# First slots of attention without the ring copy, weights' low parts on GpSimd, last feed-forward unit in two halves

## The chip, the cores and the metric

The kernel runs on one core of a Trainium2 chip. The metric is the device time of one execution in microseconds (us); the time given for a kernel is the median of several runs.
## The reference

A transformer block over 16 sequences of 256 rows and 256 features, in float32:

```
h = layernorm(x, ln1);  x = attention(h, h, sa_*) + x        # 16 heads of 64
h = layernorm(x, ln2);  x = attention(h, cond, ca_*) + x     # cond: 256 rows of 192 features
h = layernorm(x, ln3);  p = h @ ff_w1 + ff_b1                # 256 -> 2048
x = (p[:, :1024] * gelu(p[:, 1024:])) @ ff_w2 + ff_b2 + x    # 1024 -> 256
attention: softmax(q k^T / 8) v per head, heads joined, then @ wo + bo
```

## The kernel before

Each operand of a matrix product is split in two parts that the fast product format holds exactly: a high part (rounded) and a low part (the value less the high part). A product of two operands is the sum of three: high·high, high·low, low·high.

**Slots.** Both attentions are one loop of 256 slots (ATT), a slot being a pair of heads of one sequence; 128 slots for self-attention, 128 for cross-attention. The loop is written out by hand for each engine as one function per slot (`pe_slot`, `act_slot`, `dve_slot`, `pool_slot`, and the loop in the SyncE block); engines meet at semaphores only, and each works its list strictly in order. In slot c TensorE computes, in this order: scores of slot c (`pe_scores`), Q and K of slot c+3 (AHEAD, line 318), V of slot c+1 (line 294), output projection of slot c-4 (line 337), transposes of the probabilities of slot c-1 (line 350), probabilities times V of slot c-2 (line 364). ScalarE rounds Q/K (line 466) and does the exponentials (line 457) and the high part of the transposed probabilities (line 479); VectorE makes the low parts of Q/K (line 593), the negated maxima (line 557) and the low probabilities (line 545, `dve_p_low`; head 1 of slot c-2 early in the slot, head 0 of slot c-1 late); GpSimd splits V (726, 728), next sequence's rows, the output and some weights.

**The ring.** After the split, QKS holds for two heads (rows 0 to 63 and 64 to 127) the tiles K high, Q high, Q or K low. `copy_ring` copies these by four DMAs per slot to RX (lines 398 and 400), so that each head has a 128-row operand: own rows hold the head's high part, the other 64 rows the other part. With it a head's scores take two 128-row products per 128 queries (lines 280 and 281) instead of three of 64 rows. The copies for slots 1 and on are issued by SP; for slot 0 head 1 by ACT. `pe_scores` waits for them (d_dup).

**The start.** The self-attention weights come as 12 pieces of 256 KB (`PIECES`: matrix q, k or v, and quarter; `load_weights`, line 958). ScalarE rounds each into the high part (`act_weights`, line 971), VectorE makes each low part (`dve_weights`, lines 982 and 984), in numerical order, counted by s_wlo. Q/K of the first sequence wait for their pieces, V too. Slots -3 to -1 do Q/K of slots 0 to 2 and V of slot 0. TensorE runs transposes of the identity without use (`pe_warm`) at the start, before slot -3 ends and at slot 0. The second sequence's rows are normalized by VectorE in slot 0 and go through HBM; ScalarE loads them back (line 406).

**The end.** The feed-forward part has 64 units: 8 chunks (2 sequences) times 8 slices of 128 hidden features. Unit c: 12 first-layer products of 512 columns (line 828, 6 for the value half and 6 for the gate half), GELU on ScalarE (878), multiply, high and low part on VectorE (920, 924, 926); then 12 second-layer products of unit c-1 (841). After a chunk VectorE adds the residual in two halves (934) and SP stores two sequences (1052).

Of the kernel before, what the change touches and what calls it, by code (L numbers as in the profile page):

```python
# [11 lines left out]
P = 128  # L12
# [26 lines left out]
AHEAD = 3  # L39

# [34 lines left out]
def block_kernel(nc, x, ctxt, ln1_g, ln1_b, ln2_g, ln2_b, ln3_g, ln3_b, sa_wq, sa_wk, sa_wv, sa_wo,  # L75
                 sa_bo, ca_wq, ca_wk, ca_wv, ca_wo, ca_bo, ff_w1, ff_b1, ff_w2, ff_b2, out):
    ctx = ExitStack()
    with ctx:
# [75 lines left out]
        def pieces_for(m, p):  # L154

            return PIECES.index((m, p // 2)) + 1
# [18 lines left out]
        s_wlo = sem("s_wlo")  # L175
        s_ph = sem("s_ph")
# [89 lines left out]
        def pe_warm(e, times, bank=WOP):  # L266

            for _ in range(times):
                e.transpose(bank[:, S:S + P], IDN[:, :], IDN[:, :])
# [14 lines left out]
        def pe_values(e, sl, v):  # L284
# [5 lines left out]
            if v < PAIRS and v % 2 == 0:  # L290
                e.wait_ge(s_wlo, pieces_for(2, v))
# [6 lines left out]
        def pe_slot(e, sl):  # L298
            c = sl.c
            if sl.has(c + AHEAD):  # L300
# [3 lines left out]
                if k < PAIRS and k % 2 == 0:  # L304
                    e.wait_ge(s_wlo, pieces_for(1, k))
# [14 lines left out]
                last.then_inc(a.pe_qk, 1)  # L320

# [20 lines left out]
            if sl.has(c - 1):  # L342
                s = c - 1
                sl.wait(e, a.act_exp, 2 * s + 2)
                for i in range(2):
                    sl.wait(e, a.dve_pl, 2 * s + i - 1)
                    for kt in range(TT):
                        for qt in range(TT):
                            q0 = (i * TT + qt) * S + kt * P
                            last = e.transpose(PTB[:, i, kt * S + qt * P:kt * S + (qt + 1) * P],  # L350
                                               PT[:, s % 2, q0:q0 + P], IDN[:, :])
                last.then_inc(a.pe_t, 1)
# [38 lines left out]
        def copy_ring(e, k, *heads):  # L391
# [3 lines left out]
            if k >= 2:  # L395
                e.wait_ge(a.pe_s, 2 * (k - 1))
            for i in heads:
# [28 lines left out]

        def act_slot(e, sl):
# [21 lines left out]

            if sl.has(c):  # L450
                sl.wait(e, a.pe_t, c - 1)
                sl.wait(e, a.dve_rc, c - 1)
                for i in range(2):
# [6 lines left out]

            if sl.has(c + AHEAD):
                k = c + AHEAD
                sl.wait(e, a.pe_qk, k + 1)
                if k > 1:
                    e.wait_ge(d_dup[k % 2], 16 * COPIES * (k // 2))
                e.activation(QKS[:, k % 2, 0:2, :], qk_bank(k)[:, :].rearrange("p (u s) -> p u s", u=2), ACT.Copy) \  # L466
                    .then_inc(a.act_hi, 1)
# [79 lines left out]

        def dve_slot(e, sl):
# [11 lines left out]
            if c == 0:  # L560
                dve_weights(e, 6)
                e.wait_ge(a.pe_h, 2)
                dve_normalize(e, sl, a, 1, (near(1),))
# [26 lines left out]
            if sl.has(c + AHEAD):  # L590
                k = c + AHEAD
                sl.wait(e, a.act_hi, k + 1)
                e.tensor_tensor(QKS[:, k % 2, 2:4, :], qk_bank(k)[:, :].rearrange("p (u s) -> p u s", u=2),  # L593
                                QKS[:, k % 2, 0:2, :].bitcast(F32), ALU.subtract).then_inc(a.dve_lo, 1)
# [215 lines left out]

        def pe_ffn(e, sl):
# [3 lines left out]
            if sl.has(c):  # L815
# [8 lines left out]
                for g in range(2):  # L824
                    n = 0
                    for k in range(KD):
                        for wp, ap in ((0, 0), (0, 1), (1, 0)):
                            last = e.matmul(AG[c % 2][:, g, :], w1(k, wp, g * FF + f * P),  # L828
                                            rounded(chunk, ap, k), start=n == 0, stop=n == 5)
                            n += 1  # L830
                last.then_inc(fs.pe_f1, 1)

            if sl.has(c - 1):
# [3 lines left out]
                for t in range(2 * TT):  # L837
                    if f == 0 and t % 2 == 0:
# [31 lines left out]
        def act_ffn(e, sl):  # L870
            c = sl.c
            if sl.has(c):
# [3 lines left out]
                if c == 0:  # L876
                    e.wait_ge(a.pe_t, ATT)
                e.activation(FG[:, c % 2, :], AG[c % 2][:, 1, :], ACT.Gelu,
                             bias=B1[:, PAIRS + f:PAIRS + f + 1]).then_inc(fs.act_g, 1)
# [29 lines left out]

        def dve_ffn(e, sl):  # L910
# [6 lines left out]
            if sl.has(c):  # L917
# [11 lines left out]
            if f == 0 and c > 0:  # L929
                sl.wait(e, fs.pe_f2, c)  # L930
                sl.wait(e, fs.pl_xb, chunk)
                for h in range(2):
                    cols = sl.x_cols(chunk - 1, h * XW)
# [52 lines left out]
        def act_attention_slot(e, sl):  # L986
            act_slot(e, sl)
            if -AHEAD <= sl.c < 3:
                act_weights(e, *((4,), (5,), (6,), (7,), (8, 9), (10, 11))[sl.c + AHEAD])
            if sl.c == -3:  # L990
                copy_ring(e, 0, 1)
            if sl.c == -2:
                load_weights(e, 11)
# [5 lines left out]
        def dve_attention_slot(e, sl):  # L999
            c = sl.c  # L1000
            dve_slot(e, sl)
            if -AHEAD <= c < 3:
                dve_weights(e, *((4,), (5,), (), (7,), (8, 9), (10, 11))[c + AHEAD])
            if c == -2:
                dve_await_x(e, sl, 1)
# [307 lines left out]
```

## Time and profile before

| | us |
|---|---|
| median of 3 runs | 1729.74 (1728.88 to 1730.17) |
| the profiled execution | 1728.96 |
| its span | 1727.2 |
| TensorE busy | 1704.0 (99%) |
| VectorE busy | 1471.2 (85%) |
| ScalarE busy | 1184.5 (69%) |
| GpSimd busy | 1072.5 (62%) |

The span is the time from the first to the last thing the profile sees; a run's time is a little longer. Busy shares are means over the whole span; where an engine at 99% can still lose or win time is seen only in the stretches where it waits. All numbers below are from one profiled execution.

### The profile page before, as it was taken

To read this page: it belongs to the slowest core of one execution; us is meant where nothing else is said; L and a number is where in the kernel's file an instruction comes from. 1 tells how busy PE (TensorE), PEld (TensorE's weight loads), DVE (VectorE), ACT (ScalarE), POOL (GpSimd) and SP (SyncE) were. 2 spreads that over 40 slices of the span, in tenths; PEclk is the share of its full clock that TensorE was granted. 3 is DMA by queue.
4 is the path that set the end of the run, shared out by engine and by line. 5 is a ranking of instruction groups with operands and counts; after the bars stand their busy time and mean duration, and the time that the engine had idled before them with its cause. 6 is when DMAs were issued, how large, how long until landed. Compare 5 with 4: busy or idle time off the path is not lost.

```text
span 1727.2 us, 42949 instructions
## 1 busy us (share of the span) xinstructions
PE 1704.0 (99%) x13614; PEld 1664.4 (96%) x13614; DVE 1471.2 (85%) x3192; ACT 1184.5 (69%) x3244; POOL 1072.5 (62%) x1801
## 2 busy tenths in 40 slices
PE   7999999999999999999999999999999998999998
PEld 7999999999999999999999999999999997888887
DVE  6888889888888888899999999999999997666664
ACT  5777777777777777777777778777777775222221
POOL 3787777766666666787777777777777764132121
PEclk9999999999999999999999999999999999999999
DMA  8777777676666666667778777776666662212210
GB/s 224 195 181 177 181 177 179 172 182 164 154 157 152 158 154 161 169 165 186 188 189 192 191 189 182 183 180 168 169 168 168 161 168 53 74 50 70 65 37 25
DMA packets 287984, 265.95 MB, mean 154 GB/s; under 512 B 102416, under 2 KB 247696, under 8 KB 287760
## 3 DMA queue, kind: packets, MB, share of 16 engines
q1 hardware_dynamic: 232112, 248.18, 57.0%
q10 hardware_dynamic: 55648, 15.02, 4.0%
q8 instruction: 110, 1.80, 0.4%
q14 instruction: 114, 0.93, 0.2%
HBM read 70.40 MB, written 24.90 MB: 55 GB/s over the span
## 4 chain that ended last, share of the span: by engine, by line
PE 90%; DVE 2%; DMA 2%; ACT 1%; SPq 1%; POOL 1%; issue 1%; ACTq 0%; DVEq 0%; POOLq 0%
PE QKB L318 19%; PE PVB L364 13%; PE PTB L350 12%; PE WOP L337 10%; PE VB L294 9%; PE S L280 6%; PE S L281 6%; PE PTB L828 5%; PE S L828 5%; PE VB L841 3%; PE QKB L841 3%; DMA RX<-QKS 1%; ACT PT L457 1%; DVE NM L557 0%; ACT PH L479 0%
## 5 line engine op out<-in xcount | busy, mean ns | idle before, releaser
L457 ACT ACTIVATE PT<-S,NM 128x256 f32<-128x256 f32 x1024 | 471.1, 472 | 188.9 <-DVE NM L557 188.3
L545 DVE TENSOR_TENSOR PL<-PTB,PH 128x512 fp32r<-128x512 f32 x512 | 349.6, 683 | 89.7 <-ACT PH L479 84.0
L747 POOL TENSOR_TENSOR ON<-ON,RB 128x256 f32<-128x256 f32 x256 | 188.6, 737 | 283.9 <-DVE ON L573 270.5
L479 ACT ACTIVATE PH<-PTB 128x1024 fp32r<-128x1024 f32 x256 | 263.4, 1029 | 100.5 <-PE PTB L350 97.1
L557 DVE TENSOR_REDUCE NM<-S 128x2 f32<-128x512 f32 x512 | 325.8, 677 | 0.0
L350 PE MATMUL PTB<-IDN,PT 128*128 128x128 f32 x2048 | 266.7, 273 | 6.0 <-DVE PL L545 5.8
L280 PE MATMUL S<-RX 128*128 128x256 f32 x1024 | 257.1, 283 | 3.5 <-DMA RX<-QKS 3.3
L281 PE MATMUL S<-RX 128*128 128x256 f32 x1024 | 256.7, 283 | 0.0
L350 PEld LDWEIGHTS PTB<-IDN,PT 128*128 128x128 f32 x2048 | 229.4, 140 | 7.8 <-DVE PL L545 7.5
L337 PE MATMUL WOP<-WO,OT 128*128 128x256 f32 x1536 | 226.3, 283 | 1.2 <-POOL OT L752 1.2
L573 DVE TENSOR_TENSOR ON<-PVB,ON 64x256 f32<-64x256 f32 x512 | 213.3, 417 | 3.5
L457 ACT ACTIVATION_READ_ACCUMULATOR PT<-S,NM 128x1 f32 x1024 | 207.4, 203 | 0.0
L318 PE MATMUL QKB<-HT,WA 128*128 128x256 f32 x1512 | 203.6, 284 | 2.9 <-DVE WA L984 1.3
L337 PEld LDWEIGHTS WOP<-WO,OT 128*128 128x128 f32 x1536 | 202.7, 192 | 1.8 <-POOL OT L752 1.6
L439 ACT ACTIVATE ON<-PVB 64x256 f32<-64x256 f32 x512 | 193.8, 379 | 15.0 <-issue 3.0
L752 POOL TENSOR_TENSOR OT<-ON,OT 128x256 fp32r<-128x256 f32 x256 | 189.5, 740 | 20.5
L728 POOL TENSOR_TENSOR VR<-VF,VR 128x256 fp32r<-128x256 f32 x256 | 189.0, 738 | 20.5
L280 PEld LDWEIGHTS S<-RX 128*128 128x128 f32 x1024 | 195.6, 191 | 4.1 <-DMA RX<-QKS 3.6
L281 PEld LDWEIGHTS S<-RX 128*128 128x128 f32 x1024 | 196.5, 192 | 0.0
L318 PEld LDWEIGHTS QKB<-HT,WA 128*128 128x128 f32 x1512 | 191.5, 193 | 3.8 <-issue 1.9
L364 PE MATMUL PVB<-PH,VR 128*128 128x256 f32 x1024 | 183.6, 300 | 1.2 <-issue 1.1
L593 DVE TENSOR_TENSOR QKS<-QKB,QKS 128x512 fp32r<-128x512 f32 x254 | 165.7, 652 | 12.6 <-ACT QKS L466 12.3
(128 smaller groups left out, 3124.8 us busy)
## 6 DMA issues: line engine op xcount, KB each, us to landing
RX<-QKS SPq DMA_DIRECT2D x511, 192.0 KB, 2.9
RX<-QKS SPq DMA_DIRECT2D x511, 128.0 KB, 2.8
RB<-denominators SPq DMA_DIRECT2D x512, 64.0 KB, 2.6
out_dram<-XR SPq DMA_DIRECT2D x32, 256.0 KB, 2.9
rows<-XN SPq DMA_DIRECT2D x24, 256.0 KB, 2.5
rows<-HF SPq DMA_DIRECT2D x23, 256.0 KB, 2.5
XR<-in_x_dram SPq DMA_DIRECT2D x16, 256.0 KB, 3.3
denominators<-RDT SPq DMA_DIRECT2D x256, 16.0 KB
```

The source lines that it names most:

```text
L280: e.matmul(o, q, RX[:, c % 2, i, K1, :], start=True, stop=False)
L281: last = e.matmul(o, q, RX[:, c % 2, i, K2, :], start=False, stop=True)
L318: last = e.matmul(qk_bank(k)[:, m * S:(m + 1) * S], w[:, p * P:(p + 1) * P], act, start=j == 0, stop=j == len(passes) - 1)
L337: last = e.matmul(WOP[:, t * D:(t + 1) * D], OT[:, op, t * P:(t + 1) * P], WO[:, p, wp, :], start=p == 0 and t == 0 and j == 0, stop=p == ...
L350: last = e.transpose(PTB[:, i, kt * S + qt * P:kt * S + (qt + 1) * P], PT[:, s % 2, q0:q0 + P], IDN[:, :])
L364: last = e.matmul(PVB[:, i * S:(i + 1) * S], VR[:, s // 2 % 2, kt, s % 2, i * P:(i + 1) * P], part[:, first:first + S], start=i == 0 and j ...
L439: last = e.activation(ON[OWN[i], s % 2, :], PVB[OTHER[i], i * S:(i + 1) * S], ACT.Copy)
L457: last = e.activation(PT[:, c % 2, j * S:(j + 1) * S], S1[:, i, qt * S:(qt + 1) * S], ACT.Exp, bias=NM[:, j:j + 1], accum_out=DEN[:, c % 2 ...
L479: e.activation(PH[:, s % 2, :], PTB[:, :, :].rearrange("p i n -> p (i n)"), ACT.Copy) \
L545: e.tensor_tensor(PL[:, cols], PTB[:, i, :], PH[:, s % 2, cols].bitcast(F32), ALU.subtract).then_inc(a.dve_pl, 1)
L557: e.tensor_reduce(NM[:, i * TT:(i + 1) * TT], S1[:, i, :].rearrange("p (t s) -> p t s", t=TT), AX.X, ALU.max, negate=True).then_inc(a.dve_ ...
L573: last = e.tensor_tensor(on, PVB[OWN[i], i * S:(i + 1) * S], on, ALU.add)
```

## The change

Four things, all outside the steady part of the loop:

1. For the first three slots (DIRECT) the scores read QKS directly, in three 64-row products per head and 128 queries, the two heads in turn; no ring copy is made for them. Scores of slot 0 stand in slot -1, ahead of Q/K of slot 2. In slots 1 and 2, Q/K of slot c+3 go behind the transposes; the matching copy and split on ScalarE and VectorE stand before the exponentials and right after the maxima. The copy and split of slot 2 go to slot 0. The warm-up transposes of slot 0 are dropped.
2. Of the 12 low parts of weight pieces, VectorE makes five (0, 1, 3, 5, 9), GpSimd seven (2, 4, 6, 7, 8, 10, 11), in `pool_low`, with a semaphore for each engine; `await_low` picks the one to wait for.
3. High parts 4 and 5 stand before slot -3 on ScalarE, behind the issue of all pieces; the others one a slot. The second sequence's statistics, and with them its normalization (now in slot -3) and its store, come earlier.
4. The last feed-forward unit is computed in two halves of 256 columns, each with its own GELU, multiply and split; the second-layer products, the residual and the stores of the last chunk go by halves too. (Stores of every chunk wait for their own half only.)

The core of the diff:

```
+DIRECT = 3
+DVE_LOW = (0, 1, 3, 5, 9)
+POOL_LOW = (2, 4, 6, 7, 8, 10, 11)
         def pe_scores(e, sl):
             c = sl.c
-            if sl.has(c):
-                e.wait_ge(d_dup[c % 2], 16 * COPIES * (c // 2 + 1))
+            if 0 <= c < DIRECT:
+                e.wait_ge(a.dve_lo, c + 1)
+                sl.wait(e, a.act_exp, 2 * c)
+                for qt in range(TT):
+                    for j, (q, k) in enumerate(((1, 0), (1, 2), (3, 0))):
+                        for i in range(2):
+                            last = e.matmul(S1[:, i, qt * S:(qt + 1) * S],
+                                            QKS[OWN[i], c % 2, q, qt * P:(qt + 1) * P], QKS[OWN[i], c % 2, k, :],
+                                            start=j == 0, stop=j == 2)
+                            if qt == TT - 1 and j == 2:
+                                last.then_inc(a.pe_s, 1)
+            elif sl.has(c):
+                e.wait_ge(d_dup[c % 2], 16 * COPIES * ((c - 1) // 2))
...
+        def pe_slot(e, sl):
+            c = sl.c
+            late = 0 < c < DIRECT
+            if not late:
+                pe_project(e, sl)
...
+            pe_transposes(e, sl)
+
+            if late:
+                pe_project(e, sl)
...
+        def act_copy_qk(e, k):
+
+            e.wait_ge(a.pe_qk, k + 1)
+            if k > DIRECT + 1:
+                e.wait_ge(d_dup[k % 2], 16 * COPIES * ((k - 3) // 2))
+            elif k > 1:
+                e.wait_ge(a.pe_s, 2 * (k - 1))
+            e.activation(QKS[:, k % 2, 0:2, :], qk_bank(k)[:, :].rearrange("p (u s) -> p u s", u=2), ACT.Copy) \
+                .then_inc(a.act_hi, 1)
...
+            if 0 < c < DIRECT:
+                act_copy_qk(e, c + 2)
...
+            if c == 0:
+                act_copy_qk(e, 2)
+            elif sl.has(c + AHEAD) and not -1 <= c < DIRECT - 1:
+                act_copy_qk(e, c + AHEAD)
...
+            if 0 < c < DIRECT:
+                dve_split_qk(e, c + 2)
...
         def pe_attention_slot(e, sl):
-            if sl.c == 0:
-                pe_warm(e, 10, PTB[:, 1, :])
-            pe_scores(e, sl)
+            if sl.c == -1:
+                pe_scores(e, Slot(0, ATT))
+            if sl.c > 0:
+                pe_scores(e, sl)
             pe_slot(e, sl)
...
+        def pool_low(e, *ns):
+
+            for n in ns:
+                m = PIECES[n][0]
+                w = WA[:, KD * m:KD * (m + 1), :, piece_cols(n)]
+                e.wait_ge(s_whi, n + 1)
+                e.tensor_tensor(w[:, :, 1, :], raw(n), w[:, :, 0, :].bitcast(F32), ALU.subtract).then_inc(s_wlp, 1)
...
             e.wait_ge(s_ini, 1)
             pool_rstd(e, zero, a, 0)
+            pool_low(e, 2, 4)
             pool_rstd(e, zero, a, 1)
+            pool_low(e, 6, 7)
             run_slots(0, ATT + 3, ATT, lambda sl: pool_attention_slot(e, sl))
...
             act_weights(e, 2, 3)
-            load_weights(e, 8, 9, 10)
+            load_weights(e, 8, 9, 10, 11)
+            act_weights(e, 4, 5)
...
-            dve_weights(e, 2, 3)
+            dve_weights(e, 3)
+            dve_await_x(e, zero, 1)
+            dve_stats(e, zero, a, 1)
+            dve_aggregate(e, zero, a, 1)
+            dve_weights(e, 5)
...
+                if c == FU - 1:
+                    pe_ffn_first(e, chunk, f, 0).then_inc(fs.pe_f1, 1)
+                    pe_ffn_first(e, chunk, f, 1).then_inc(fs.pe_f1, 1)
...
                 for t in range(2 * TT):
+                    if s == FU - 1 and t == TT:
+                        last.then_inc(fs.pe_f2, 1)
+                        e.wait_ge(fs.dve_hl, FU + 1)
...
+        def dve_ffn_half(e, h):
+
+            r, f, cols = (FU - 1) % 2, PAIRS - 1, slice(h * S, (h + 1) * S)
+            e.wait_ge(fs.act_g, FU + h)
+            e.scalar_tensor_tensor(FV[:, r, cols], last_half(h)[:, 0:S], B1[:, f:f + 1], FG[:, r, cols],
+                                   ALU.add, ALU.mult).then_inc(fs.dve_hf, 1)
```

## Rows read from the trace of the kernel before

**Rows 1.** The page, part 1: busy us, share of the span, instructions.
```profile
PE 1704.0 (99%) x13614; PEld 1664.4 (96%) x13614; DVE 1471.2 (85%) x3192; ACT 1184.5 (69%) x3244; POOL 1072.5 (62%) x1801
```

**Rows 2.** Waits of PE, 0 to 40 us: total, times, longest.
```profile
PE S L280 <- DMA RX<-QKS: 3.3, 1, 3.3
PE PTB L350 <- DVE PL L545: 2.2, 1, 2.2
PE QKB L318 <- DVE WA L984: 1.3, 1, 1.3
```

**Rows 3.** Stretches: length, busy PE, PEld, DVE, ACT, POOL; PE clock; DMA; GB/s.
```profile
9.33:39.06 29.73, 22.11 (x162) 20.84 (x162) 19.92 (x42) 15.83 (x42) 10.12 (x18) 0.94 0.83 226
...
20.40:22.60 2.20, 2.20 (x12) 2.20 (x12) 2.20 (x6) 1.48 (x7) 0.00 (x0) 0.50 0.96 294
...
35.20:37.00 1.80, 1.78 (x15) 1.79 (x16) 1.15 (x4) 1.80 (x6) 1.14 (x2) 1.00 0.65 195
```

**Rows 4.** Chain of waits, 8 to 50 us: start, length, what.
```profile
8.76 0.43 DVE HT L519
...
9.33 1.69 PE QKB L318 x12
...
11.04 0.61 ACT QKS L466
...
11.67 0.70 DVE QKS L593
...
13.00 6.09 DMA RX<-QKS
...
47.31 0.87 PE PTB L350 x8
...
49.14 0.12 PE S L280
```

**Rows 5.** Timeline of ACT and its queue: start, length, what.
```profile
8.08 1.16 ACT L971 ACTIVATE WA<-PT 128x512 fp32r<-128x512 f32 x2
...
9.03 0.49 ACTq L958 DMA_DIRECT2D XR<-in_L_xattn_sa_wq_dram  x1
...
26.91 0.47 ACT L457 ACTIVATE PT<-S,NM 128x256 f32<-128x256 f32 x1 [2.72 <-DVE NM L557]
...
29.30 2.06 ACTq L406 DMA_DIRECT2D HF<-rows  x3
```

**Rows 6.** Piece 5's issue on SP's queue; DMA issues to 15 us: KB, us to landing.
```profile
4.79 0.48 SPq L958 DMA_DIRECT2D STG<-in_L_xattn_sa_wq_dram  x1
...
STG<-in_L_xattn_sa_wq_dram SPq DMA_DIRECT2D x1, 256.0 KB, 5.2
```

**Rows 7.** Timelines of DVE and POOL, 25 to 29 us.
```profile
25.28 0.99 DVE L984 TENSOR_TENSOR WA<-XR,WA 128x512 fp32r<-128x512 f32 x1
...
25.67 0.86 POOL L677 CAST WO<-RB 128x256 fp32r<-128x256 f32 x1
...
28.92 0.73 POOL L728 TENSOR_TENSOR VR<-VF,VR 128x256 fp32r<-128x256 f32 x1
```

**Rows 8.** Chain of waits, the end of the kernel.
```profile
1715.16 2.76 PE PTB L828 x12
...
1717.95 0.70 ACT PT L878
...
1718.67 0.76 DVE PT L920
...
1719.46 0.44 DVE HT L924
...
1719.92 0.70 DVE HT L926
...
1720.67 0.98 PE QKB L841 x6
...
1722.45 0.69 DVE XR L934
```

More of the change, by code:

```diff
@@ L175, in block_kernel @@
         s_wlo = sem("s_wlo")
+        s_wlp = sem("s_wlp")
         s_ph = sem("s_ph")
@@ L320, in pe_slot, with pe_transposes @@
                 last.then_inc(a.pe_qk, 1)
+        def pe_transposes(e, sl):
+            c = sl.c
+            if sl.has(c - 1):
+                s = c - 1
+                sl.wait(e, a.act_exp, 2 * s + 2)
+                for i in range(2):
+                    sl.wait(e, a.dve_pl, 2 * s + i - 1)
+                    for kt in range(TT):
+                        for qt in range(TT):
+                            q0 = (i * TT + qt) * S + kt * P
+                            last = e.transpose(PTB[:, i, kt * S + qt * P:kt * S + (qt + 1) * P],
+                                               PT[:, s % 2, q0:q0 + P], IDN[:, :])
+                last.then_inc(a.pe_t, 1)
+        def pe_slot(e, sl):
+            c = sl.c
+            late = 0 < c < DIRECT
+            if not late:
+                pe_project(e, sl)
             if c >= 0 and sl.has(c + 1):
@@ L340, in pe_slot @@
                 last.then_inc(a.pe_wo, 1)
[L342 to L352, printed above, removed]
+            pe_transposes(e, sl)
+            if late:
+                pe_project(e, sl)
             if sl.has(c - 2):
@@ L389, in act_gain_bias, with copy_ring @@
                          scale=LNG[:, n // B, 0, k:k + 1]).then_inc(a.act_hf, 1)
-        def copy_ring(e, k, *heads):
+        def copy_ring(e, k):
             r, done = k % 2, d_dup[k % 2]
             e.wait_ge(a.dve_lo, k + 1)
-            if k >= 2:
-                e.wait_ge(a.pe_s, 2 * (k - 1))
-            for i in heads:
+            e.wait_ge(a.pe_s, 2 * (k - 1))
+            for i in range(2):
                 e.dma_start(RX[OWN[i], r, i, :, :].bitcast(F32), QKS[OWN[i], r, 0:3, :].bitcast(F32)) \
@@ L588, in dve_slot @@
                 e.transpose(RDT[:, c % 2, :], RDEN[:, :]).then_inc(a.dve_rt, 1)
[L590 to L594, printed above, removed]
+            if c == 0:
+                dve_split_qk(e, 2)
+            elif sl.has(c + AHEAD) and not -1 <= c < DIRECT - 1:
+                dve_split_qk(e, c + AHEAD)
             if prepares and pair == 2:
@@ L809, in w2, with last_half, pe_ffn_first @@
             return WA[:, 4 + f // 4, part, (f % 4) * D:(f % 4 + 1) * D]
+        def last_half(h):
+            return AG[(FU - 1) % 2][:, h, :]
+        def pe_ffn_first(e, chunk, f, h):
+            cols = slice(h * S, (h + 1) * S)
+            for g in range(2):
+                n = 0
+                for k in range(KD):
+                    for wp, ap in ((0, 0), (0, 1), (1, 0)):
+                        last = e.matmul(last_half(h)[:, g * S:(g + 1) * S], w1(k, wp, g * FF + f * P),
+                                        rounded(chunk, ap, k)[:, cols], start=n == 0, stop=n == 5)
+                        n += 1
+            return last
         def pe_ffn(e, sl):
@@ L823, in pe_ffn @@
                     e.wait_ge(a.dve_pl, 2 * ATT)
[L824 to L831, printed above, removed]
+                if c == FU - 1:
+                    pe_ffn_first(e, chunk, f, 0).then_inc(fs.pe_f1, 1)
+                    pe_ffn_first(e, chunk, f, 1).then_inc(fs.pe_f1, 1)
+                else:
+                    for g in range(2):
+                        n = 0
+                        for k in range(KD):
+                            for wp, ap in ((0, 0), (0, 1), (1, 0)):
+                                last = e.matmul(AG[c % 2][:, g, :], w1(k, wp, g * FF + f * P),
+                                                rounded(chunk, ap, k), start=n == 0, stop=n == 5)
+                                n += 1
+                    last.then_inc(fs.pe_f1, 1)
             if sl.has(c - 1):
@@ L916, in dve_ffn @@
                 e.wait_ge(a.pe_qk, ATT)
-            if sl.has(c):
+            if c == FU - 1:
+                sl.wait(e, fs.pe_f2, c - 1)
+                dve_ffn_half(e, 0)
+                dve_ffn_half(e, 1)
+            elif sl.has(c):
                 r = c % 2
@@ L932, in dve_ffn @@
                 for h in range(2):
+                    if c == FU and h:
+                        e.wait_ge(fs.pe_f2, FU + 1)
                     cols = sl.x_cols(chunk - 1, h * XW)
@@ L1208, in _ @@
                     load_ffn_rows(e, chunk + 1, *range(8))
-                e.wait_ge(fs.dve_xo, PAIRS * (chunk + 1))
-                for b in (2 * chunk, 2 * chunk + 1):
-                    save_x(b)
+                for h in range(2):
+                    e.wait_ge(fs.dve_xo, PAIRS * chunk + PAIRS // 2 * (h + 1))
+                    save_x(2 * chunk + h)
                 if chunk < NCK // 2:
```

86 lines of the change are left out of this document (48 added, 38 removed).

## The prediction

> **What bounds the kernel now.** Start with the page: TensorE (PE) is busy 99% of the span [rows 1], so only its idle or slowed time can be won back, or work added to it. The waits of PE over the first 40 us name three holes: 3.3 us for the ring copy before the first scores, 2.2 us in the transposes of slot 1, 1.3 us for a weight's low part [rows 2]. The table by stretches puts a sum on that stretch: from the first Q/K product (9.33) to that of slot 3 (39.06), 29.73 us, PE is busy 22.11 [rows 3]. After 3.3 us without work its granted clock is 0.50 of full (1.2 GHz) at 20.4 to 22.6 [rows 3], so part of the busy time is slow too. The chain of waits gives the start in order: Q/K product, ACT copy 0.61, DVE split 0.70, ring copies, of which the last lands after 6.09 us at 19.09, then scores; further down it gives block prices at full clock, a product of 256 columns every 0.12, 8 transposes in 0.87 [rows 4]. By these a steady slot is scores 0.96, Q/K 1.44, V 0.72, output 0.72, transposes 0.87, P·V 0.96: 5.67 us, all PE. At 100 us and beyond nothing in the change touches the order; what counts is by how much slot 5's scores (49.14 [rows 4]) move, and the tail.
>
> I write QK(k), V(k), S(k), T(k), PV(k) for PE's blocks of slot k; high(n) and low(n) for the two parts of weight piece n.
>
> **The start, step by step.** All times are the profiled execution's.
> 1. ACT has one more DMA issue and high(4), high(5) ahead of the first copy. Four issues of 0.49 from 8.62 end at 10.58; two weight copies of 0.53 to their successor (1.16 for two, the last 0.63) end the queue at 11.64 [rows 5]. Piece 5 is issued at 4.79 and its landing comes after 5.2 us, at 10.0 [rows 6], so data is no wait. The copy of slot 0 runs 11.64 to 12.25, 0.6 later than in [rows 4]; DVE, behind low(5), splits 12.35 to 13.05.
> 2. S(0) no longer waits for the ring: 13.06 instead of 19.13. This is +6.1.
> 3. POOL now runs low(2) beside DVE's splitting of the first rows and low(4) beside low(5). POOL shows no 512-column subtraction; 256 columns take 0.73 [rows 7], so I put 1.42 (fixed part counted twice at most: 1.46; if slowed as below, 2.0). Where a DVE and a POOL operation, both reading SBUF, overlapped, DVE took 0.99 (0.70 is what such a subtraction takes in [rows 4]) and POOL's cast 0.86, where its two-operand subtraction of the same size takes 0.73 [rows 7]. Two such meetings lie on the path to S(0): between 0 and 0.6, I take 0.4. Low(4) ends near 12.65, the reciprocal root follows by 13.64, DVE's normalization by 14.4, the split of slot 1 by 15.0.
> 4. Direct scores are 12 products of 64 rows, no such row in this trace. Serial they cost 12 × 0.12 = 1.44; if the two heads' products, on different rows and banks, run side by side, 0.72. Taken: 1.2, nearer the known pitch. Against 0.96 that is +0.24 in each of three slots (−0.24 to +0.48).
> 5. QK(2), QK(3), V(1) follow: 1.44 + 1.44 + 0.72. Meanwhile DVE reduces from 15.3, ACT's four exponentials (0.45 apart, 0.47 each [rows 5]) end at 17.97, S(1) starts at 17.99: no hole.
> 6. S(1) 1.2, V(2) 0.72, T(0) 0.87 reach 20.78. QK(4), now behind T(0), waits for the split of slot 3. That split needs S(1) done (19.35), the ACT copy (to 19.98) and two maxima on DVE ahead of it: 21.20. Hole 0.4.
> 7. QK(4) to 22.66, S(2) to 23.86, V(3), first half of T(1) to 25.0. Its second half waits for the low probabilities of slot 0, head 1, which DVE does after two maxima and the split of slot 4: 24.08 + 3 × 0.60 + 0.69 = 26.57 (a start every 0.60: the 0.70 of [rows 4], less the 0.1 by which DVE's successive operations overlap). Hole 1.6; this is the new late thing. ACT's four row loads (0.39 + 2.06 in the trace [rows 5]) stand ahead of high(10) and the copy of slot 4, but end at 23.6, just covered by S(2). If they were 1 us later, T(1) would be too.
> 8. Rest of T(1) 0.43, QK(5) 1.44, PV(0) 0.96: S(3) at 29.43. The ring copies of slot 3 are issued from 21.2 (four issues, 2.5 us) and even with the 6.09 of [rows 4] land by 29.8, so 0 to 0.4; normally hidden. QK(6) at 30.39; its weights are done (low(9) at 24.2, low(10) at 25.7).
> 9. With the 0.4 of step 3: 30.8 instead of 39.06, 8.3 earlier. The waits of [rows 2] and the half clock are gone, because no hole is over 1.6 us: after the hole of 2.2 us the trace shows the clock at 1.00 from 35.2 on [rows 3].
> 10. POOL takes seven low parts in place of DVE. It reaches slot 3 late, since low(11) waits for high(11) behind the probabilities' copy (30.7) and ends at 32.1; V split, next sequence's low part, bias and output scaling follow until 37.7, when PE wants the output of slot 0. A hole of 0.2 to 0.5. Afterwards POOL has about 5 us of work in a slot of 5.67 and catches up.
>
> Start: 8.3 − 0.3 = **8.0 us**. The warm-up transposes of slot 0 stood in a hole; dropping them is worth nothing. SP's waits on pieces 6 to 11 stand before x loads of much later sequences: nothing.
>
> Aside from this sum: the Trainium skill ("TensorE: Matmul & The Clock Gate", Part 3) has products on different row groups run concurrently, which by itself gives the 0.72 of step 4 and some 0.3 us more gain; "TensorEngine Tiling (Array Packing)", Key Properties, says that a change of tiling mode drains the engine, which speaks for the serial end; no row of before shows either. For step 3, [rows 7] agree with the Trainium skill's "GPSIMD Reference", 1. Specifications, that POOL contends with DVE instructions which have two SBUF inputs: by that rule more of the early low parts than my two would be slowed, and the sum would lose up to 2 us.
>
> **The tail.** Before: last product ends 1717.92, then GELU 0.70, multiply 0.76, cast 0.44, subtraction 0.70, 12 products (0.98 for the first six), two sums of 0.69, two stores [rows 8]; the span ends at 1727.2, 3.5 after the last sum. After: the unit's first products are 24 × 0.12 = 2.88 for 2.76 [rows 8] (+0.13). Halves of 256 columns cost GELU 0.48, multiply 0.49, cast 0.29, subtraction 0.42 (each less about 256 × 1.05 ns, from 0.70 and the 0.43 at 8.76 in [rows 4]). First half ready at 1716.6, low part 1718.4; PE is busy with the unit before until 1719.32, so this is hidden. Second half: product ends 1718.05, GELU 1718.55, low part 1719.83, its six products after the first half's six, 1720.04 to 1720.93; sum 1721.67; one store with 3.0 left of the 3.5 (one issue of 0.45 fewer): 1724.7. **2.5 us** (2.2 if the halves cost as much as whole operations in their fixed parts, 2.9 if the lone store lands faster).
>
> **Sum.** 8.0 + 2.5 = 10.5. The profiled execution took 1728.96 us (span 1727.2), the median of the runs is 1729.74, 0.78 above it. So 1718.5 for a profiled run, and 1729.74 − 10.5 = **1719.2** as the time. Own range of this case 1717.3 to 1721: pairs of products at 0.72 and no contention add 1.0, the store 0.4; serial products and POOL parts of 2.0 take 2.0.
>
> **Rivals.**
> - *The start turns POOL- or ACT-bound.* For it: one POOL operation at double price, 11 us in which POOL formerly stood idle now filled, high(4), high(5) before the first copy. Worked through with low parts of 2.8 and direct scores of 1.8, slot 5 moves by only 3.0: total 5.5, 1724.2. Should piece 5 land only where the trace first shows it used (14.46), S(0) is 2.9 later: total 7.6, 1722.1. Against: the landing in [rows 6], and a POOL that is idle until 8.7.
> - *Clock.* The half clock of 20.4 to 22.6 followed a hole. If 64-row products, or the row of short holes, left PE at 1.2 GHz, each us of work costs 2. From S(0) to QK(6) there are about 15 us of work: +15 against 10.5 won, 1734, slower. It decides from 10.5 us of work at half clock. Against: from 9.33 on PE has no hole until 20.8.
> - *The ring was not the bound.* If removing the copy only uncovers exponentials, DVE and the holes of slots 1 and 2 grow by as much, just the tail is left: 1727.2. Against: DVE loses seven low parts (0.60 each, 4.2 us) and was busy only 19.9 of 29.7 [rows 3].
>
> **Chances.** Forecast (1717 to 1721) 0.66; start bound by POOL, ACT or late data (1721 to 1725.5) 0.20; more than forecast (below 1717) 0.06; only the tail 0.04; clock 0.04. Faster by over 0.2% (3.5 us, about what this kernel's measurement can tell) 0.92, within it 0.04, slower 0.04. Range 1716.2 to 1723.6.
>
> **What would show it.** In the profile after: first score products at 13.1 to 13.6; a pitch of the 64-row products between 0.06 and 0.12; no granted clock near 0.5 before 40 us; a PE wait of 1 to 2 us in the transposes on the low probabilities and one below 0.6 in QK on the split; slot 3's ring copies no releaser of PE; QK of slot 3 near 30.8; POOL's 512-column parts at 1.4 to 2.0; one sum and one store after the last product, 1.6 to 2.9 us shorter than before. I am wrong if S(0) starts after 15, if a hole over 3 us stays, or if POOL releases PE for more than 1 us after slot 3.

## The result, and the profile after

The changed kernel takes 1720.12 us (median of 4, 1719.67 to 1720.45) against 1729.95 on the same occasion: ratio 0.9943, 95% interval 0.9926 to 0.996, 9.8 us faster. Forecast was 1719.2, range 1716.2 to 1723.6. Run once more in a later job, the same kernel took 1721.09 (5 runs, 1720.65 to 1722.16) against 1729.39: 8.3 us. Its profiled execution took 1720.33, span 1718.5, so 8.6 less than the one of before.

The page of the changed kernel, span and part 1, answers to [rows 1]:

```profile
span 1718.5 us, 42973 instructions
...
PE 1701.5 (99%) x13628; PEld 1663.3 (97%) x13628; DVE 1470.9 (86%) x3188; ACT 1186.7 (69%) x3245; POOL 1082.9 (63%) x1808
```

Its waits of PE from 0 to 50 us (total, times, longest) answer to [rows 2]:

```profile
PE S L290 <- ACT PT L507: 1.7, 1, 1.7
...
PE PTB L355 <- DVE PL L592: 1.3, 1, 1.3
PE S L290 <- DVE QKS L598: 0.8, 1, 0.8
```

The ring copy and the weight's low part are gone as releasers; the low probabilities remain, and there are two new holes (stretches without work) before the direct scores (line 290), of 0.8 in slot 0 and 1.7 in slot 1. The stretches answer to [rows 3]:

```profile
19.20:20.80 1.60, 0.00 (x0) 0.00 (x0) 0.62 (x3) 1.60 (x9) 1.60 (x3) 1.00 0.00 0
...
22.20:23.60 1.40, 1.40 (x8) 1.40 (x8) 1.35 (x3) 1.16 (x4) 1.27 (x3) 0.50 0.08 12
```

After the hole the granted clock is 0.50 again, as in [rows 3]. The chain of waits of the changed kernel, start and middle, in place of [rows 4]:

```profile
13.80 0.73 POOL RSTD L677
...
14.63 2.59 DVE XN L556 x2
17.23 0.60 DVE QKS L598
...
20.87 1.33 PE S L290 x12
...
30.80 1.43 PE QKB L341 x12
...
34.14 1.44 PE QKB L341 x12
...
44.28 0.12 PE S L302
```

Read it upwards from the last row: slot 5's scores stand at 44.28 where they stood at 49.14 [rows 4], so the start has won 4.9 us. (Their first products start 0.16 earlier, at 44.12 and 48.98; below, such first starts are compared.) The Q/K rows are those of slot 2 (30.80) and slot 3 (34.14). What carries the chain from 14.6 to 20.9 is VectorE's normalization, two operations in 2.59 us. The end of the chain answers to [rows 8]:

```profile
1709.22 2.88 PE PTB L872 x24
...
1713.54 0.73 PE QKB L914 x6
...
1714.35 0.69 DVE XR L1032
...
1715.08 0.69 DVE XR L1032
```

From the first product of the last unit to the end it is now 1718.45 − 1709.22 = 9.2 us; it was 1727.2 − 1715.16 = 12.0 [rows 8]. So 2.8 of the span's 8.7 us come from the tail and 4.9 from the start. The remaining 1.0 arose in between, in code that the change does not touch, and is looked at under "The change once more".

### The profile page after: what moved, and what is told of

Its sections match the earlier page's. It is cut to its first block, busy times and chain, and to the rows that moved or that the text cites. A ratio compares the mean times of both kernels' runs of the same rounds, so it can differ in the third digit from the quotient of the medians.

```text
span 1718.5 us, 42973 instructions
## 1 busy us (share of the span) xinstructions
PE 1701.5 (99%) x13628; PEld 1663.3 (97%) x13628; DVE 1470.9 (86%) x3188; ACT 1186.7 (69%) x3245; POOL 1082.9 (63%) x1808
## 4 chain that ended last, share of the span: by engine, by line
PE 94%; DVE 2%; ACT 1%; POOL 1%; DMA 1%; issue 1%; SPq 1%; ACTq 0%; POOLq 0%; DVEq 0%
PE QKB L341 19%; PE PVB L400 14%; PE PTB L355 12%; PE WOP L380 10%; PE VB L316 9%; PE S L303 7%; PE S L302 7%; PE S L898 5%; PE PTB L898 5%; PE QKB L914 3%; PE VB L914 3%; ACT PT L507 0%; DVE NM L610 0%; ACT PH L526 0%; DVE PL L592 0%
## 5 line engine op out<-in xcount | busy, mean ns | idle before, releaser
L302 PE MATMUL S<-RX 128*128 128x256 f32 x1012 | 253.7, 283 | 0.0
L303 PE MATMUL S<-RX 128*128 128x256 f32 x1012 | 253.7, 283 | 0.0
L303 PEld LDWEIGHTS S<-RX 128*128 128x128 f32 x1012 | 194.3, 192 | 0.0
L302 PEld LDWEIGHTS S<-RX 128*128 128x128 f32 x1012 | 193.4, 191 | 0.0
L598 DVE TENSOR_TENSOR QKS<-QKB,QKS 128x512 fp32r<-128x512 f32 x254 | 165.9, 653 | 13.1 <-ACT QKS L469 13.0
```

What stands on the lines that cost most here:

```text
L302: e.matmul(o, q, RX[:, c % 2, i, K1, :], start=True, stop=False)
L303: last = e.matmul(o, q, RX[:, c % 2, i, K2, :], start=False, stop=True)
```

## The experiments

**Tail undone.** The last unit is whole again; the rest is the changed kernel.

```
-                if c == FU - 1:
-                    pe_ffn_first(e, chunk, f, 0).then_inc(fs.pe_f1, 1)
-                    pe_ffn_first(e, chunk, f, 1).then_inc(fs.pe_f1, 1)
-                else:
+                if True:
...                      (GELU, dve_ffn_half, second-layer and residual halves likewise)
```

> The change without its last part: the last feed-forward unit is computed whole, as before. If the tail is worth what the two traces show (2.8 us from the first product of the last unit to the end: 12.04 before, 9.28 after), this kernel takes 1722.9 (1720.1 + 2.8), and its trace has the chain GELU 0.70, multiply, cast, subtraction, 12 products, two sums, two stores again. Rival: the halves only move work and the later end is set by the stores' landing; then it takes within 1 us of 1720.1.

Measured 1723.11 (before 1729.73 in that job): 3.0 above the changed kernel. PE's one wait at the end is the whole low part again:

```profile
PE QKB L908 <- DVE HT L1006: 1.3, 1, 1.3
```

In the traces, too, the stretch from the last unit's first product to the end is 2.9 us longer (12.3 for 9.4). The tail's price is shown; the rival falls.

**The ring kept, low parts on GpSimd.** DIRECT = 0, scores, copies and splits in the old order, ring copies for all slots. It is not quite the old start: the warm-up transposes of slot 0 stay out, the high parts and the second sequence's normalization keep their new places, and SP issues all four copies of slot 0.

> The change with the ring copies of slots 0 to 2 and the old order of their scores, copies and splits (DIRECT = 0), the low parts on GpSimd kept. If the ring was the bound of the start, the scores of slot 0 start at 18 to 20 us and nearly the whole gain of the start (5.9 us) is lost: 1725.5 to 1727. Rival, that relieving VectorE of seven low parts (4.2 us of it) is what shortened the start: scores of slot 0 as late, but slots 1 to 3 closer together and 1722 to 1723.5.

Measured 1724.52 (1723.52 to 1726.46): 4.4 above the changed kernel, between the two expectations. PE waits for the ring copies again (total, times, longest), and for 6.8 us around them, twice as long as in the kernel before, the clock is low:

```profile
PE S L302 <- DMA RX<-QKS: 4.5, 2, 3.5
```

```profile
16.80:23.50 6.70, 5.15 (x24) 5.15 (x25) 2.68 (x5) 3.05 (x10) 2.40 (x3) 0.50 0.90 215
```

Slot 5's scores start at 47.08: 1.9 earlier than before, and 3.0 to 3.6 later than in the changed kernel (44.12, 43.73 in its second trace, 43.51 in the kernel with the whole last unit, which starts alike). Another 1.0 of the 4.4 lies at the change to the feed-forward part, where the clock fell in this trace (see the transposes below); whether it fell in the other executions too is not known.

**All low parts on VectorE, scores direct.** POOL_LOW empty; VectorE makes 2 and 4 before slot -3, then 6, 7, 8, 9 in slots -2 to 1, 10 and 11 in slot 2.

```
-            dve_weights(e, 5)
+            dve_weights(e, 4, 5)
...
-            if c == 1:
-                dve_weights(e, 9)
+            if -2 <= c <= 2:
+                dve_weights(e, *((6,), (7,), (8,), (9,), (10, 11))[c + 2])
```

> The change with all twelve low parts on VectorE, none on GpSimd. Theory (GpSimd's low parts slow VectorE's operations beside them: normalization of the second sequence's rows 2.59 us for two operations instead of 0.73): these take 0.73 again, the split of slot 1 comes at about 15.5 instead of 17.15, the scores of slot 1 at 19.5 to 20.5 instead of 20.87, while the low parts cost VectorE 4.2 us later; total within 1 us of 1720.1, or up to 2 us faster. Rival (moving the low parts to GpSimd is worth its 4.2 us on the path): 1722 to 1724.

Measured 1722.57. Both were partly right. The mechanism is the theory's: with GpSimd quiet, the low part of piece 3 and the normalization take their usual time. The timeline of VectorE in this kernel:

```profile
9.95 0.69 DVE L1081 SCALAR_TENSOR_TENSOR WA<-PT,WA 128x512 fp32r<-128x512 f32 x1
...
14.77 0.73 DVE L556 TENSOR_SCALAR XN<-XR,MV,RSTD 128x256 f32<-128x256 f32 x2
```

But they do not make it faster: low parts 2 and 4 now stand ahead of the split of slot 0 (its scores wait 1.7), 6 and 7 ahead of the maxima (scores of slot 1 at 20.35, where three traces of the changed start have 20.20 to 20.87), and Q/K of slot 6 waits for low part 10:

```profile
PE QKB L341 <- DVE WA L1083: 1.3, 1, 1.3
```

The median is 2.5 above the changed kernel's (1719.96 to 1723.94, the profiled execution the slowest). In the trace, slot 5's scores (44.88) are 0.8 to 1.4 later; 1.3 more is a fall of the clock at the change to the feed-forward part, and the rest lies in slots 128 to 180, which differ from one execution to the next. So of the rival's price only 0.8 to 1.4 is shown to come from the low parts.

By the three runs, then: direct scores 3.0 to 3.6 us, the low parts on GpSimd about 1 beside direct scores, the tail 2.9. Beside the ring, all else that is new before slot 5 (low and high parts, the second sequence's rows, no warm-up) wins 1.9 together. These do not add up by themselves: what one part wins depends on which wait the others leave.

**What GpSimd does to VectorE.** The same instructions in the timelines of DVE and then POOL of the changed kernel:

```profile
9.75 1.46 DVE L1081 SCALAR_TENSOR_TENSOR WA<-PT,WA 128x512 fp32r<-128x512 f32 x1 [0.23 <-ACT WA L1070]
...
11.66 0.75 DVE L537 BATCH_NORM_STATS2 ST<-XR 128x6 f32<-128x256 f32 x2 [0.46 <-DMA XR<-in_x_dram]
...
12.62 1.02 DVE L1081 SCALAR_TENSOR_TENSOR WA<-STG,WA 128x512 fp32r<-128x512 f32 x1
...
14.63 2.59 DVE L556 TENSOR_SCALAR XN<-XR,MV,RSTD 128x256 f32<-128x256 f32 x2 [0.39 <-POOL RSTD L677]
...
18.08 1.27 DVE L610 TENSOR_REDUCE NM<-S 128x2 f32<-128x512 f32 x2
...
28.81 0.68 DVE L598 TENSOR_TENSOR QKS<-QKB,QKS 128x512 fp32r<-128x512 f32 x1
```

```profile
9.11 1.55 POOL L1126 TENSOR_TENSOR WA<-PT,WA 128x512 fp32r<-128x512 f32 x1 [3.23 <-ACT WA L1070]
...
11.78 1.31 POOL L1126 TENSOR_TENSOR WA<-STG,WA 128x512 fp32r<-128x512 f32 x1 [1.13 <-ACT WA L1070]
...
14.49 2.58 POOL L1126 TENSOR_TENSOR WA<-XR,WA 128x512 fp32r<-128x512 f32 x2
...
18.70 0.74 POOL L778 TENSOR_TENSOR VR<-VF,VR 128x256 fp32r<-128x256 f32 x1
...
28.20 1.28 POOL L1126 TENSOR_TENSOR WA<-XR,WA 128x512 fp32r<-128x512 f32 x1 [4.07 <-ACT WA L1070]
```

Low part 3 (9.75), low part 5 (12.62) and the normalization (14.63) each end soon after GpSimd's subtraction beside them: 11.21 after 10.66, 13.64 after 13.09, 17.22 after 17.07. They are held, not slowed. In the eleven traces with low parts on GpSimd there are 22 meetings in which VectorE's 512-column subtraction starts second; it took 1.00 to 1.79 us, by how long GpSimd's still ran, and ended 0.55 after GpSimd's in all 22. Not held are the statistics (11.66, one input from SBUF), the maxima (18.08, from PSUM), and a split with one input from PSUM (28.81): they take their usual time beside GpSimd's subtraction. (So not everything but the products works in SBUF alone: VectorE reads PSUM as well.)

Where VectorE starts first, GpSimd is the one held. Low part 9 on VectorE, then low part 10 on GpSimd, in the kernel "GpSimd moved instead" below:

```profile
24.56 0.76 DVE L1081 SCALAR_TENSOR_TENSOR WA<-XR,WA 128x512 fp32r<-128x512 f32 x1
```

```profile
24.93 1.53 POOL L1126 TENSOR_TENSOR WA<-XR,WA 128x512 fp32r<-128x512 f32 x1 [0.16 <-ACT WA L1070]
```

VectorE keeps its time and GpSimd takes 1.53 instead of 1.28. The 1.55 at 9.11 above is the same case: a subtraction of VectorE had started at 9.09. The Trainium skill ("GPSIMD Engine Reference", 1. Specifications) names contention with VectorE instructions of two SBUF inputs or a two-port mode. For the subtractions, which read two tensors of SBUF, the trace agrees: low part 3 takes 1.46 instead of 0.69. The normalization reads one such tensor (and two values per row), and no row tells its mode.

**Normalization moved to slot 0**, behind the maxima, as in the kernel before.

```
-            if c == -AHEAD:
-                e.wait_ge(a.pe_h, 2)
-                dve_normalize(e, sl, a, 1, (near(1),))
...                      (now in dve_slot)
+            if c == 0:
+                e.wait_ge(a.pe_h, 2)
+                dve_normalize(e, sl, a, 1, (near(1),))
```

> The change with one edit: VectorE normalizes the second sequence's rows in slot 0, behind the maxima, and no longer ahead of the split of slot 1. Theory (the 1.7 us hole before the scores of slot 1, and the half clock of 4 us behind it, come from these two operations standing ahead of split, V copy and maxima): split of slot 1 at 14.3, exponentials from 16.0, no hole before the scores of slot 1 (19.0), granted clock 1.00 throughout, TensorE 2.5 to 3.3 us ahead at slot 3: 1717 to 1718. Rival (the exponentials are late for other reasons, or the low probabilities in slot 2 take the gain back): 1719 to 1720.1.

Measured 1721.23 (1719.06 to 1721.66). The hole before slot 1's scores is gone (they start at 18.94), as the theory had it, and the next one took it all back (scores of slot 3 at 33.98, where the changed kernel has 33.02): with everything earlier, low part 9 on VectorE meets GpSimd's low part 10. VectorE's row in its timeline, then GpSimd's:

```profile
24.56 1.79 DVE L1085 SCALAR_TENSOR_TENSOR WA<-XR,WA 128x512 fp32r<-128x512 f32 x1
```

```profile
24.52 1.28 POOL L1127 TENSOR_TENSOR WA<-XR,WA 128x512 fp32r<-128x512 f32 x1 [1.45 <-ACT WA L1074]
```

PE's wait (total, times, longest), and the stretch behind it, with the clock at 0.51:

```profile
PE PTB L355 <- DVE PL L592: 2.6, 1, 2.6
```

```profile
28.00:30.00 2.00, 1.20 (x6) 1.21 (x7) 1.42 (x5) 1.00 (x5) 1.62 (x3) 0.51 0.46 108
```

**GpSimd moved instead.** The changed kernel, with `pool_low(e, 6, 7)` behind the split of V in slot 0.

> The changed kernel with GpSimd's low parts 6 and 7 behind its split of V of slot 0, so that nothing runs on GpSimd beside VectorE's normalization. Theory (held by GpSimd): the two normalizing operations take 0.73 instead of 2.59, the split of slot 1 comes at 15.4, exponentials from about 17.0, scores of slot 1 at 18.9 to 19.2 with no hole; V of slot 2, which needs low 7, waits for it to about 20.3 in its place. Net 0.3 to 1.2 us ahead at slot 3. Rival (the two operations are slow by themselves, from their place before slot -2): 2.59 stays, and nothing changes before slot 1.

Measured 1719.12 (1718.98 to 1721.39), 2.0 less than the changed kernel in the same job (1721.09, 1720.65 to 1722.16); one of its four executions lies among those of the changed kernel. The two operations of the normalization, not touched themselves, take 0.74, the scores of slot 1 start at 18.96, and V of slot 2 waits 0.2:

```profile
14.59 0.74 DVE L556 TENSOR_SCALAR XN<-XR,MV,RSTD 128x256 f32<-128x256 f32 x2 [0.39 <-POOL RSTD L677]
```

So it is GpSimd's operation beside it, not the place of the normalization, that made the hole. P·V of slot 0 comes 2.0 us before that of the changed kernel in the same job, and the clock stays at 1.00.

**Low part 9 moved too**, to slot 2 ahead of the split of slot 5; then **both low probabilities of slot 0 at the end of slot 1**; then **low part 5 behind the split of slot 0**. Each on top of the one before it:

```
+            if c == 2:
+                dve_weights(e, 9)             (low part 9)
...
+                if c == 1:
+                    dve_p_low(e, 0, 1)        (low probabilities)
...
+            if c == -AHEAD:
+                dve_weights(e, 5)             (low part 5)
```

> As rows_normalized_in_slot0, and VectorE makes low part 9 in slot 2, ahead of the split of slot 5, where it stood idle 1.4 us, instead of at the end of slot 1, beside GpSimd's low part 10. Theory (a VectorE operation with its operands in SBUF is held as long as a GpSimd subtraction runs: low 9 took 1.79 us there and put the maxima of slot 2 at 26.3): maxima of slot 2 from 25.0, the hole in the transposes of slot 1 falls from 2.6 to 1.2 to 1.5 us, the clock stays at 1.00, scores of slot 3 about 2 to 2.5 us earlier than in the changed kernel: 1717.5 to 1718.5. Rival (the low part costs its 0.6 to 1.8 us wherever it stands, or what is won is lost again at slot 3 to GpSimd's output scaling): 1719.5 to 1721.

> As the kernel before it, and VectorE makes both low probabilities of slot 0 at the end of slot 1, ahead of the maxima of slot 2. Theory (that operation, behind two maxima and a split, is the hole in the transposes of slot 1): the hole goes, 0 to 0.3 us left, maxima of slot 2 0.3 later; another 1.0 to 1.4 us: 1716.3 to 1717.5. Rival (the next wait takes its place at once, ScalarE's copy and split of slot 5 or the output of slot 0 on GpSimd): the same time as the kernel before it within 0.4 us.

> As the kernel with both low probabilities early, and VectorE makes low part 5 behind the split of slot 0 instead of ahead of it (Q/K of slot 4 is the first to need it). Theory (low 5 is held by GpSimd's low 4 and stands in front of the split for which the first scores wait): split of slot 0 at 12.8 instead of 13.6, hole before the first scores 0 to 0.2 us instead of 0.8 to 1.3, all slots from 0 on 0.8 to 1.0 us earlier at slot 3; in the median 1718.5 to 1719.2 if later waits leave it. Rival (what is won before slot 3 goes back to the ring copies at the starts of sequences, whose waits differ by 1 to 2 us from one execution to the next): slot 3 is 4 us ahead of the changed kernel's, the end less than 1.5 us.

Measured 1719.69, 1719.51 and 1718.29 (1717.06 to 1719.96; the changed kernel 1720.65 to 1722.16 in the last one's job, whose profiled execution, at 1719.96, is its slowest). At the start every edit did what its theory said: P·V of slot 0 starts at 29.75, 28.73 and 27.73, where the changed kernel has 32.06. At the end of the span only 0.9, 0.9 and 0.3 of these 2.3, 3.3 and 4.3 us are left, and the times of the first two lie where their rivals put them, that of the third just below its theory's. For the first the mechanism is not its rival's: it is still 2.5 ahead at slot 128, and loses 1.4 in slots 144 to 180, which no edit touches. The other two lose 0.8 and 1.3 in slot 3 already. Where the last one's went first, PE's wait in slot 3, and POOL's (35 to 45 us):

```profile
PE WOP L380 <- POOL OT L810: 1.1, 1, 1.1
...
POOL WO L735 <- DMA STG<-in_L_xattn_sa_wo_dram: 1.6, 1, 1.6
```

GpSimd now waits for the second half of the output weights, which SP issues in slot 3, and PE waits for the output that GpSimd scales behind it. Between P·V of slots 2 and 24 the three kernels take 124.5, 126.8 and 127.6 us, the changed kernel 124.5 in its first trace and 126.1 in its second; so beyond slot 3 their loss is of the size by which one program's executions differ. The last is the fastest version here: 2.8 us below the changed kernel in the median, and its slowest execution is below the changed kernel's fastest.

**Transposes in the hole.**

```
+            if sl.c == 1:
+                pe_warm(e, 14, PTB[:, 1, :])
             if sl.c > 0:
                 pe_scores(e, sl)
```

> The changed kernel with 14 transposes of the identity, without use, in the hole ahead of the scores of slot 1 (19.2 to 20.8). They change no other engine. Theory (the half clock from 21.5 to 24.6 follows the hole and costs 1.5 us): clock 1.00 throughout, V of slot 2, transposes and Q/K of slot 4 at full pace, scores of slot 2 1.3 to 1.6 us earlier; as the maxima of slot 1 set the split of slot 3 and this the Q/K of slot 4 in part, 0.8 to 1.5 us arrive: 1718.6 to 1719.4. Rival (the slow products lie beside VectorE's and ScalarE's chain, which sets the next wait anyway): 1720.1 within 0.4.

Measured 1723.04 (1722.35 to 1724.34): slower than either text. The start went as the theory had it (clock 1.00 from 18 to 30 us, P·V of slot 0 at 31.25, 0.8 earlier). But it lost more than that elsewhere: 1.5 in slots 3 to 24 (a second trace of the changed kernel loses as much there), 1.6 in slots 144 to 180, and 1.2 at the change to the feed-forward part, where the clock fell here, and in the changed kernel did not. The stretch of this kernel, then the changed kernel's:

```profile
1445.00:1448.00 3.00, 3.00 (x14) 2.79 (x13) 0.84 (x2) 1.90 (x4) 1.84 (x3) 0.56 0.09 31
```

```profile
1443.00:1446.00 3.00, 3.00 (x18) 2.63 (x19) 1.83 (x4) 2.65 (x4) 1.71 (x3) 1.00 0.09 30
```

Ahead of both stands the same pair of holes (0.85 and 1.32). Slots 180 to 255 are 1.0 to 1.3 us longer where the clock falls, in three of the thirteen traces (the ring kept, all low parts on VectorE, and this). At the start it is the same: the clock fell behind a hole of 1.67 in the changed kernel, and not behind holes of 1.67 and 1.70 with all low parts on VectorE. That kernel's stretches behind its two holes:

```profile
14.80:19.40 4.60, 4.60 (x42) 4.36 (x42) 4.04 (x8) 1.28 (x6) 1.52 (x2) 1.00 0.54 179
29.80:33.60 3.80, 3.80 (x32) 3.69 (x32) 1.67 (x5) 1.88 (x5) 1.13 (x2) 1.00 0.84 199
```

Whether a hole of this size costs the clock is not settled by its length; what settles it was not found.

**Heads one after the other** in the direct scores.

```
-                    for j, (q, k) in enumerate(((1, 0), (1, 2), (3, 0))):
-                        for i in range(2):
+                    for i in range(2):
+                        for j, (q, k) in enumerate(((1, 0), (1, 2), (3, 0))):
```

> The changed kernel with the loops over head and product exchanged in the direct scores: three 64-row products of one head in a row, then three of the other, instead of the heads in turn. 12 products take 0.91 in the changed kernel (0.076 each). Theory (products on different rows run side by side when they alternate): they take 1.3 to 1.45 for 12, 0.12 each; up to 0.45 in each of three slots, of which 0.5 to 1.2 arrive: 1720.6 to 1721.3. Rival (a 64-row product is simply shorter): 0.91 as before and 1720.1.

Measured 1720.4 (1720.07 to 1723.82). Twelve products take the same, in the changed kernel and in this one (next block 0.91 and 0.92 after the first product):

```profile
14.29 0.98 PE L290 MATMUL S<-QKS 64*128 64x256 f32 x12 [0.82 <-DVE QKS L598]
```

```profile
13.87 0.99 PE L290 MATMUL S<-QKS 64*128 64x256 f32 x12 [0.73 <-DVE QKS L598]
```

The rival's number came out, 0.91, but not its reason. A 64-row product is not shorter: its median is 0.28 us, as for 128 rows. The products start in pairs. The same timelines, cut to 14.29 to 14.31 and to 13.87 to 13.89, show two each:

```profile
14.29 0.39 PE L290 MATMUL S<-QKS 64*128 64x256 f32 x2 [0.82 <-DVE QKS L598]
```

```profile
13.87 0.39 PE L290 MATMUL S<-QKS 64*128 64x256 f32 x2 [0.73 <-DVE QKS L598]
```

At full clock the two of a pair start 0.002 to 0.017 us apart and the pairs in a block every 0.11 to 0.13, the pitch of single 128-row products (0.12). So two do run side by side, in both orders. The record of a product does not say which rows it uses; with the heads one after the other, therefore, it stays open whether the pairs are of one head, or the engine takes the other head's product ahead.

Six pairs would be 0.72. What makes the block longer is the change of shape: from the first pair to the second it is 0.22, from the last to the next block 0.21, and the 128-row products on the far side of each change are 0.21 and 0.22 apart instead of 0.12. Counted with these, the direct scores of slot 2 cost 1.1 us (one pitch behind the last Q/K product, 26.43, to one before V's second, 27.54), against 0.96 by the ring.

**The change once more.**

> The changed kernel itself, to see on the same chip how far e9 is from it and how much one program's executions differ: 1720.1 within 0.8 in the median; the first 120 slots from slot 3 on as before within 0.3 us, the stretch of slots 144 to 180 anywhere from 195.9 to 198 us.

(In this text e9 is the kernel with low part 5 moved.) Measured 1721.09, 0.2 outside what was expected; and slots 3 to 24 took 1.6 us more than in the first trace, where 0.3 was expected. Slots 25 to 128 take 581.77 or 581.78 us in all thirteen traces. Slots 144 to 180, where no kernel differs, take 197.9 before, 196.4 in both traces of the changed kernel and 195.9 to 197.9 in the others (197.5 in the whole-unit kernel, whose code is the changed kernel's up to there); the surplus lies at the first slots of sequences, where ScalarE's copy waits for the ring copies up to 2 us. So executions differ by 1 to 2 us in stretches that nobody edited, and the 1.0 us that was open above is of this size: some 1.6 won in slots 144 to 180, 0.8 lost in slots 128 to 144, 0.2 won before slot 25, 0.1 behind slot 180. One thing speaks for a hand of the change in it: slots 128 to 144 take 87.9 in the one trace of before and 88.2 to 89.0 in all twelve others. That was not followed up.

## Why the prediction was right, and where it was off

**The time** came out closer than its parts, and that is in part luck. The forecast was 10.5 us, 8.0 from the start and 2.5 from the tail; the traces have 4.9 and 2.8, together 7.7. Another 1.0 of the span came from slots that the change does not touch, and the medians of that occasion lie 9.8 apart where the profiled spans lie 8.7; on the later occasion it was 8.3. For a profiled execution the forecast was 1718.5, and it took 1720.33. The mechanism was right (the ring copy was the first bound, the low probabilities are the next wait); the sizes of the start were not.

**Step 3 is the one that was mis-sized.** It put the contention (one engine's operation made longer by the other's) at 0.4 (0 to 0.6), at two meetings ahead of the first scores, each a slowing of at most 0.3. Measured were 0.3 for low part 5 and, at a meeting that it did not name, 1.86 for the normalization beside low parts 6 and 7; low part 3 took 0.8 more as well, but VectorE then stood idle for the second sequence's rows, so this cost nothing. Together 2.2 on the path for 0.4. The split of slot 1 was forecast to end by 15.0 and started at 17.15. With low parts 6 and 7 moved away and nothing else, slot 5's scores start at 41.75, 7.2 earlier than before: most of the 8.0. The sentence on what the rule of the Trainium skill ("GPSIMD Engine Reference", 1. Specifications) would cost ("up to 2 us") had the size; the sum did not.

**Steps 1 and 2, right with 0.8 more.** The scores of slot 0 start at 14.29, not 13.1 to 13.6. The step had ScalarE's copy as the last thing before the split. That copy was 0.5 late (12.13, as its DMA issues waited for high part 3) but done at 12.71; the split waited for VectorE itself, which got the second sequence's rows at 11.66 (a wait that the step leaves out), then did the statistics and low part 5, held to 13.64. With low part 5 moved, the split starts at 12.64 and the scores at 13.35. The limit "wrong if after 15" held: 4.8 instead of 6.1 us.

**Step 5, wrong in consequence of step 3:** "no hole" became 1.67 us before slot 1's scores (20.87 for 17.99).

**Step 9, wrong on the clock.** "No hole is over 1.6 us" became 1.67, and the clock fell to 0.50; but holes of 1.67 and 1.70 elsewhere, and the 2.2 of before, left it at 1.00, so the step's rule, that length decides, is not borne out either way. Scores of slot 1, V of slot 2 and transposes of slot 0 took some 1.3 us more (Q/K of slot 4 starts at 24.92; in the kernel with the transposes PE is ready for it at 23.63). Part of it lay beside VectorE's chain: without the fall, slot 0's P·V is 0.8 earlier (transposes in the hole). Q/K of slot 3, forecast near 30.8, starts at 33.98.

**Step 4, close:** 1.1 for 1.2. The pairs at a pitch of 0.12 are the step's cheap end (0.72); the change of shape adds about 0.4, not serial products. What the cheap end would give is stated twice, as 1.0 (with no contention) in the range and as some 0.3 beside the sum, and worked out in neither place; three blocks at 0.72 instead of 1.2 are 1.44 of PE's work.

**Steps 6 to 8, right:** the low probabilities are the next wait, 1.3 for 1.6; the ring copies of slot 3 are no releaser. The hole of 0.4 in Q/K of slot 4 is hidden by the slow clock ahead of it, and shows (0.3) where the clock stays up. **Step 10, right in kind:** no wait for GpSimd in slot 3 or 4 of the changed kernel's first trace, since all else is later, and 0.2 in its second; it is 1.1 in the version that is 4 us earlier.

**The tail:** 2.8 (2.9 by the experiment's trace) instead of 2.5, with the unit's first products at 2.88 as forecast. The 0.3 is the store: the span ends 2.7 after the last sum, not 3.0. The halves' prices agree with the trace (GELU 0.47, multiply 0.49, cast 0.30, subtraction 0.42), though the deduction given for them (256 × 1.05 ns off the whole operation) would make the GELU 0.43 and the cast 0.17.

**The rivals:** the start was bound neither by POOL nor by ACT as such but by VectorE held through GpSimd; the clock rival's mechanism occurred for about 3 us, not for 10.5; "only the tail" is refuted by the ring kept (slot 5 is 3.0 to 3.6 later).

## What to carry to other kernels

When work goes to a second vector engine, list what the first one runs at that moment: of two subtractions on SBUF that meet, the one that started second waited here for the other, and moving the neighbour of one operation on the path won 2 us. Ask also whether the held operation is waited for: low part 3 was held by 0.8 us, and it cost nothing. Each hole that is closed brings the next wait forward, so read the following releaser before pricing the gain. Where one program's executions differ by 1 to 2 us in a stretch that nobody edited, compare stretches, not totals.

## What the runs showed of the hardware

- Products of 64 rows and 256 columns start in pairs, a pair every 0.11 to 0.13 us, which is the pitch of single 128-row products; with the heads in turn or one after the other, twelve take 0.91 and 0.92. Each change between 64 and 128 rows costs about 0.2 us more.
- A VectorE subtraction on SBUF that starts during GpSimd's 512-column subtraction ends 0.55 us after it (0.69 becomes 1.00 to 1.79, 22 meetings); two normalizing operations (0.74 together) become 2.59. GpSimd's, started second, takes 1.53 instead of 1.28. Maxima and splits that read PSUM, and statistics with one SBUF input, are not held.
- After the hole of 1.67 us ahead of slot 1's scores the clock fell to 0.50 in both traces of the changed kernel and in the two that share its start; after holes of 1.67 and 1.70 it did not with all low parts on VectorE. After the pair of holes of 0.85 and 1.32 at the change of parts it fell in three traces and not in ten.
